# Block-local attention with global tokens: probabilities turned by SyncE's transposing DMAs, weighed two steps later, scores in two PSUM tiles, V in three pieces

## The reference

```python
# x: 4 x 1024 x 1024; 16 heads of 64; block 128; key window 256
h = layernorm(x)
q, k, v = h @ Wq + bq, h @ Wk + bk, h @ Wv + bv
# local: query block i sees keys 128*i - 64 .. 128*i + 192 (cut at the ends)
probs = softmax(q_block @ k_window.T / 8);  ctx = probs @ v_window
# global: row 0, row 1023 and the 62 rows of largest |q| of each head see all keys
g_ctx = softmax(q[idx] @ k.T / 8) @ v;      ctx[idx] = g_ctx
x = x + ctx
x = x + layernorm(x) @ (weight * scale_weight[:, None]).T + bias
```

## Time and profile before

| | us |
|---|---|
| median of 3 runs | 2138.94 (2134.4 to 2142.42) |
| profiled execution | 2139.94 |
| its span (first to last instruction) | 2138.4 |
| TensorE busy | 2105.3 (98%) |
| VectorE busy | 1347.3 (63%) |
| ScalarE busy | 750.6 (35%) |
| GpSimd busy | 502.7 (24%) |

### The profile page before, as it was taken

One profiled execution on the slowest core, in us unless ns is written; L12 is line 12 of the kernel. 1 busy time (PEld: TensorE's weight loads), 2 busy tenths in 40 slices (PEclk: granted clock), 3 DMA queues, 4 the chain that ended last, 5 costly groups with the idle time before them and its releaser, 6 DMA issues.

```text
span 2138.4 us, 36665 instructions
## 1 busy us (share of the span) xinstructions
PE 2105.3 (98%) x12576; PEld 1794.5 (84%) x12576; DVE 1347.3 (63%) x2615; ACT 750.6 (35%) x1915; POOL 502.7 (24%) x336
## 2 busy tenths in 40 slices
PE   6999999999999999999999999999999999999999
PEld 6878888888788888887888888888888888888887
DVE  5686666546966665459656655496555566666664
ACT  4334344442344344432444445224434451000000
POOL 2231121123411221243112311432123112212121
PEclk9999999999999999999999999999999999999999
DMA  4333232223332322233322221323223113333331
GB/s 161 104 95 92 75 104 67 61 69 99 107 90 75 106 60 65 69 95 93 98 85 77 84 70 42 103 65 86 65 68 123 51 58 134 140 131 134 137 128 69
DMA packets 192506, 194.29 MB, mean 91 GB/s; under 512 B 91984, under 2 KB 157590, under 8 KB 192400
## 3 DMA queue, kind: packets, MB, share of 16 engines
q1 hardware_dynamic: 184752, 175.19, 27.7%
q10 hardware_dynamic: 4320, 15.73, 1.8%
q0 software_dynamic: 3328, 2.17, 0.6%
HBM read 122.73 MB, written 51.44 MB: 81 GB/s over the span
## 4 chain that ended last, share of the span: by engine, by line
PE 85%; DVE 11%; issue 2%; DMA 1%; ACT 1%; DVEq 0%; SPq 0%; POOL 0%; ACTq 0%; POOLq 0%
PE proj L566 40%; PE proj L742 15%; PE pv L691 10%; PE score L664 5%; PE turn L679 5%; PE pv L722 3%; DVE top_idx L1307 2%; DVE x_norm L1309 2%; PE score L704 2%; DVE top_val L1305 2%; DVE q_sq L1272 2%; PE turn L714 1%; PE turn L731 1%; PE proj L831 1%; DVE norms L1274 1%
## 5 line engine op out<-in xcount | busy, mean ns | idle before, releaser
L566 PE MATMUL proj<-xT_hi,w_lo 128*128 128x512 f32 x1536 | 409.6, 398 | 0.0
L566 PE MATMUL proj<-xT_hi,w_hi 128*128 128x512 f32 x1536 | 402.7, 404 | 2.5 <-issue 1.5
L566 PE MATMUL proj<-xT_lo,w_hi 128*128 128x512 f32 x1536 | 381.5, 390 | 0.0
L434 POOL CAST w_hi<-w_raw 128x1024 fp32r<-128x1024 f32 x96 | 100.7, 1049 | 1178.4 <-PE proj L566 910.3
L566 PEld LDWEIGHTS proj<-xT_lo,w_hi 128*128 128x128 f32 x1536 | 288.6, 188 | 63.1
L566 PEld LDWEIGHTS proj<-xT_hi,w_lo 128*128 128x128 f32 x1536 | 281.1, 188 | 62.2 <-issue 0.2
L566 PEld LDWEIGHTS proj<-xT_hi,w_hi 128*128 128x128 f32 x1536 | 274.2, 188 | 63.4 <-DVE kT_lo L1290 2.7
L994 ACT ACTIVATE probs<-score,neg_max 128x256 f32<-128x256 f32 (+1 forms) x512 | 229.2, 460 | 183.4 <-DVE neg_max L1363 122.5
L691 PEld LDWEIGHTS pv<-v_nat,pT 128*128 128x128 f32 x2048 | 248.1, 191 | 10.4
L691 PE MATMUL pv<-v_nat,pT 128*128 128x64 f32 x2048 | 242.3, 271 | 0.0
L436 POOL TENSOR_TENSOR w_lo<-w_raw,w_hi 128x1024 fp32r<-128x1024 f32 x96 | 232.4, 2421 | 7.8
(11 more groups left out here) (165 smaller groups left out, 2975.0 us busy)
## 6 DMA issues: line engine op xcount, KB each, us to landing
w_raw<-in_wstream SPq DMA_DIRECT2D x96, 512.0 KB
x_buf<-in_rows SPq DMA_DIRECT2D x55, 512.0 KB, 4.1
q_rows<-q_nat SPq DMA_DIRECT2D x64, 256.0 KB
ctx_rows<-ctx_out SPq DMA_DIRECT2D x128, 128.0 KB, 1.8
q_store<-ctx_rows SPq DMA_DIRECT2D x30, 512.0 KB
out<-q_store ACTq DMA_DIRECT2D x30, 512.0 KB, 2.6
q_store<-in_cols SPq DMA_DIRECT2D x28, 512.0 KB
q_store<-in_rows SPq DMA_DIRECT2D x8, 512.0 KB, 5.3
```

What stands on the lines that cost most here:

```text
L434: pool.tensor_copy(w_hi[b][:, :], w_raw[b][:, :]).then_inc(w_hi_set, 1)
L566: mm = pe.matmul(proj[:, bank, :], w[b][:, k * P:k * P + P], x[:, k, half * HALF:half * HALF + HALF], start=(m == 0), stop=(m == 23), skip ...
```

## The change

**Turning.** TensorE's transposes of probabilities are gone, and with them ScalarE's copies out of `turn`. In their place, for each of the five events and each half (ten times a unit): VectorE splits the probabilities into 16-bit halves (`part_p`), SyncE issues a transposing DMA (`turn_p`, which is now SyncE's), and ScalarE joins the two halves into `pT` (`join_p`). `pT` becomes three tiles: two that alternate over the steps and `pT_g` for the global event. The buffers for it come from reuse: `v_parts` lies in `q_sq`, `q_nat` and `qT_cur` in the two `pT`.

**Order on TensorE.** A step is weighed about two steps after its scores. The weighings of step 3 and of the global event stand in the next unit. The scores of steps 1 and 3 go to the PSUM tile `turn`, which is free now; those of 0 and 2 to `score`.

**V and banks.** V goes in three equal pieces of 3 tiles each (`V_PIECES = 3`), all three joined within the second step. The parts of a unit come in the order V, V, K, K (V, K, V, K in unit 6), and each 512-token half has a seat (bank and count) given by `seat`: the first halves of V and K in bank 0, the second ones in bank 1, in most units.

**SyncE.** In `stores`, the loads of rows (units 0 and 1), of the last column (unit 2) and the linear layer's first loads (last batch, unit 7) stand between the transposes of step 1 and step 2; before, the row loads were the last of the unit. The store of step 3's context moves into the next unit, and the saving of the row statistics behind the last transposes of unit 3.

**VectorE.** The row moments stand in the middle of the unit instead of near its end; `SCALE_AT`, `LO_AT`, `HI_AT` and `AHEAD_AT` give other places.

The core of the diff:

```diff
+        v_parts = q_sq[:, 0:3 * P].bitcast(U16).rearrange("p (s x) -> p s x", s=2)
+        v_turned = sb("v_turned", [P, 3, 2, 3 * P], U16)
         v_nat = sb("v_nat", [P, TILES + 1, 2, HD])
-        probs = sb("probs", [P, SEQ])
-        pT = sb("pT", [P, SEQ + P])
+        probs = sb("probs", [P, SEQ + P])
+        p_parts, p_turned = (sb(name, [P, 2 * (SEQ + P)], U16) for name in ("p_parts", "p_turned"))
+        pT = [sb(f"pT{b}", [P, SEQ]) for b in range(2)]
+        pT_g = sb("pT_g", [P, SEQ + P])
+        q_nat, qT_cur = pT[0][:, :].rearrange("p (t d) -> p t d", d=P), pT[1]
...
+        score_of = [score, turn, score, turn]
...
+        V_PIECES = 3
+        V_NEEDS = (1, 2, 3, 3)
+
+
+        def half_words(s, h):
+
+            return slice(h * HALF, h * HALF + HALF + (P if s == STEPS and h == 1 else 0))
+
+
+        def pT_of(s):
+            return pT_g if s == STEPS else pT[s % 2]
+
+
+        BANK_USES = (SLICES + 1, SLICES - 1)
+
+
+        def seat_q(i, half):
+
+            return (1 - i, half) if i < 2 else (half, i)
+
+
+        def seat(what, j, half):
+
+            if isinstance(j, int) and j == 0:
+                return (0 if what == "v" else 1), PAIRS + half
+            if isinstance(j, int) and j == PAIRS - 1:
+                if what == "v":
+                    return 0, 3 * PAIRS - 2 + half
+                return ((1, 3 * PAIRS - 2), (0, 3 * PAIRS))[half]
+            return half, 2 * j + PAIRS + (0 if what == "v" else 1)
...
-        SCALE_AT = {(4, 1): (0,), (4, 2): (1,), (4, 3): (2,), (4, 6): (3,), (5, 1): (4,), (5, 2): (5,), (5, 3): (6,), (6, 1): (7,)}
+        SCALE_AT = {(4, 0): (0,), (4, 2): (1,), (4, 3): (2,), (5, 0): (3,), (5, 2): (4,), (5, 3): (5,), (6, 0): (6,), (6, 1): (7,)}
...
+            def turn_p(n, hp, s):
+
+                i = n * (PAIRS * EVENTS) + hp * EVENTS + s
+                for h in range(2):
+                    words = half_words(s, h)
+                    sp.wait_ge(p_parted, 2 * i + h + 3)
+                    apart(sp)
+                    sp.wait_ge(pT_set, 2 * i + h + 1)
+                    apart(sp)
+                    sp.dma_start_transpose(p_turned[:, 2 * words.start:2 * words.stop].rearrange("p (x r) -> p x r", r=P),
+                                           p_parts[:, 2 * words.start:2 * words.stop]).then_inc(p_moved[h], 16)
...
+                turn_p(n, hp, 0)
+                if hp > 0:
+                    store_ctx(n, hp - 1, STEPS - 1)
+                turn_p(n, hp, 1)
+                if hp == HALF_PAIRS + 1 and not following:
+                    load_ahead_next()
+                if hp < 2 and following:
+                    load_rows(n, hp + 2)
+                if hp == 2:
+                    load_last_column(n, following)
+                if last and not following:
+                    load_first()
+                turn_p(n, hp, 2)
                 store_ctx(n, hp, 0)
-                if hp < PAIRS - 1:
+                if not last:
                     turn_v(n, hp + 1, 0)
-                if hp == PAIRS - 1 and not following:
-                    load_first()
-                store_ctx(n, hp, 1)
                 if next_slices:
                     sp.wait_ge(w_split[1], n * BUFS + PAIRS // 2 + 3 + hp)
                     sp.dma_start(w_raw[1][:, :], next_slices[1]).then_inc(raw_in[1], 16)
+                turn_p(n, hp, 3)
+                store_ctx(n, hp, 1)
+                if not last:
+                    turn_v(n, hp + 1, 1)
+                turn_p(n, hp, STEPS)
                 store_ctx(n, hp, 2)
+                if not last:
+                    turn_v(n, hp + 1, 2)
                 if hp == HALF_PAIRS - 1 and following:
                     save_stats(n)
-                store_ctx(n, hp, 3)
-                if hp < PAIRS - 1:
-                    turn_v(n, hp + 1, 1)
+                if hp == HALF_PAIRS + 1 and not following:
+                    load_bias()
+                if last:
+                    store_ctx(n, hp, STEPS - 1)
...
-            def turn_p(u, s):
-                for h in range(2):
-                    pe.wait_ge(exp_set, 2 * (u * EVENTS + s) + h + 1)
-                    if s == 0:
-                        apart(pe)
...
-                            mm = pe.transpose(turn[0:rows, col:col + P], probs[:, src:src + rows], ident[:, :])
-                    mm.then_inc(p_turned, 1)
...
             def weigh(u, s):
                 pe.wait_ge(pv_free, u * EVENTS + s + 1)
-                if s < 2:
-                    pe.wait_ge(v_set, 2 * u + s + 1)
+                pe.wait_ge(v_set, u * V_PIECES + V_PIECES + V_NEEDS[s])
                 for h in range(2):
-                    pe.wait_ge(pT_set, 2 * (u * EVENTS + s) + h + 1)
+                    pe.wait_ge(pT_set, u * (2 * EVENTS) + 2 * s + h + 3)
...
+            def attend(n, hp):
                 u = n * PAIRS + hp
...
+                opens = isinstance(hp, int) and hp == 0
+                early = isinstance(hp, int) and hp == PAIRS - 2
+                scores(n, hp, 0)
+                part_of(n, hp, 0)
+                if not opens:
+                    weigh(u - 1, 3)
+                part_of(n, hp, 1)
+                scores(n, hp, 1)
+                if not opens:
+                    global_weigh(u - 1)
+                part_of(n, hp, 2)
+                scores(n, hp, 2)
+                part_of(n, hp, 3)
+                weigh(u, 0)
+                part_of(n, hp, 4)
+                scores(n, hp, 3)
+                turn_gq(u)
+                part_of(n, hp, 5)
+                weigh(u, 1)
+                if not early:
+                    part_of(n, hp, 6)
...
+                weigh(u, 2)
+                if early:
+                    part_of(n, hp, 6)
...
+            def join_p(n, hp, s, h):
+
+                i = n * (PAIRS * EVENTS) + hp * EVENTS + s
+                words = half_words(s, h)
+                act.wait_ge(p_moved[h], 16 * i + 32)
+                if s in (2, 3):
+                    act.wait_ge(pv_done, i - 1)
+                elif isinstance(hp, int) and hp == 0 and s == 0:
+                    act.wait_ge(q_stored[h], n * (16 * PAIRS) + 16 * PAIRS + 16)
+                    act.wait_ge(q_squared[h], n * PAIRS + PAIRS + 1)
+                apart(act)
+                act.copy(pT_of(s)[:, words].bitcast(U16).rearrange("p (x s) -> p s x", s=2),
+                         p_turned[:, 2 * words.start:2 * words.stop].rearrange("p (s x) -> p s x", s=2)).then_inc(pT_set, 1)
...
+                exps(u, 3, 0)
+                gq_hi_out(u)
+                before(3, 0)
+                exps(u, 3, 1)
+                before(3, 1)
+                if not last:
+                    out("v", 1, 2)
...
+            def part_p(n, hp, s, h):
+
+                i = n * (PAIRS * EVENTS) + hp * EVENTS + s
+                words = half_words(s, h)
+                dve.wait_ge(exp_set, 2 * i + h + 3)
+                dve.wait_ge(p_moved[h], 16 * i + 16)
                 apart(dve)
-                dve.tensor_copy(v_nat[:, V_TILES[h], :, :].rearrange("p t h d -> p (t h d)").bitcast(U16)
-                                .rearrange("p (t r s) -> p t s r", r=P, s=2), v_turned[:, V_TILES[h], :, :]).then_inc(v_set, 1)
+                dve.tensor_copy(p_parts[:, 2 * words.start:2 * words.stop].rearrange("p (s x) -> p s x", s=2),
+                                probs[:, words].bitcast(U16).rearrange("p (x s) -> p s x", s=2)).then_inc(p_parted, 1)
...
+                join_v(n, hp, 0)
+                top_norms(2)
+                part_p(n, hp, 1, 1)
+                inverses(u, 1)
+                for k in range(1, V_PIECES):
+                    join_v(n, hp, k)
...
+                part_p(n, hp, 2, 0)
+                top_norms(3)
+                pad_q(n, u, hp, half)
+                pv_out(u, 0)
+                part_p(n, hp, 2, 1)
+                inverses(u, 2)
+                if following and hp < HALF_PAIRS - 1:
+                    row_moments(n, hp + 1)
                 columns(2)
+                maxima(u, 3)
+                if not last:
+                    split_q(u + 1, hp + 1)
+                part_p(n, hp, 3, 0)
+                gq_lo_out(u)
+                if ahead:
+                    out_ahead(1, 0)
+                top_norms(4)
                 pv_out(u, 1)
-                if ahead:
-                    out_ahead(0, 0)
-                maxima(u, 3)
-                inverses(u, 2)
-                pad_q(n, u, hp, half)
-                top_norms(3)
+                part_p(n, hp, 3, 1)
+                inverses(u, 3)
+                if not last:
+                    part_v(n, hp + 1, 1)
```

677 lines of the change are left out of this document (357 added, 320 removed).

## The result

| | before | changed |
|---|---|---|
| median, us | 2138.0 (4 runs) | 2258.6 (2256.7 to 2263.5, 4 runs) |
| ratio, 95% interval | | 1.057 (1.054 to 1.059) |
| profiled execution, span | 2139.9, 2138.4 | 2260.1, 2258.4 |

What follows compares the result with a forecast made beforehand. TensorE's own work was taken to bound the kernel, end to end. From 2139.9 us, less 154.2 and 7.1, plus 24, 42, 9 and 11, came 2064.7, less 1 for the median: 2064 us, range 2035 to 2095.

Steps and rivals of the forecast that it cites:

- (a): TensorE's part after the second weighing waits for V's copy behind ScalarE's joins: 1.0 us in 24 units, 24 us.
- VectorE's term: VectorE gains ten splittings, loses 1 us in V's pieces: 32.4 us busy in a unit of 36.6, 88% full.
- (b): Units 0 to 2, first three batches: row loads ahead of third step's transposes in SyncE's queue; 42 us besides (a).
- What goes: TensorE's transposes of probabilities, 4.8 us a unit, 154.2 in all, and 7.1 us of waits at them.
- splittings at 0.69: VectorE's ten splittings of probabilities a unit, priced by its fast 1024-element row at 0.69 us each.
- joins at 1.0: ScalarE's ten joins a unit, priced between 0.6 and 1.12, taken as 1.0 us (0.95 back to back).
- The round trip: Splitting, DMA and join between scores and weighing: 8 us needed, about 17 available, so the weighing doesn't wait.
- (c): Unit 4, first three batches: late spreading of row statistics delays VectorE's scaling and maxima; 3 us more than (a), 9 us.
- The hand order: VectorE's operations in order with the forecast's prices; in unit 4 it waits until about 12 us in.
- VectorE sets the pace: Rival: VectorE, 88% full, has late maxima; each unit loses 1.5 us more, 48 us, time 2112; chance 0.15.
- transposes in series: Rival: transposing DMAs don't overlap, 3 us each, making a unit 44.5 us, time 2239; chance 0.08.

Runs made afterwards that it cites:

- e2: Changed kernel, ScalarE's copy of V's second half moved ahead of step 3's exponentials in units 0 to 6: 2193.8 us, ratio 1.027.
- e12: Changed kernel, GpSimd's subtraction for the weights' low parts in eight instructions of 128 columns instead of one of 1024: 2224.0 us, ratio 1.042.
- e9: Changed kernel, GpSimd's subtraction for V's and K's weight slices cut to 64 of 1024 columns, the rest left out: 2230.7 us, ratio 1.044.
- the better version: e8's kernel, roots and statistics store as in the changed kernel, unit 4's spreading load and first column scalings placed otherwise: 2182.4 us, ratio 1.021.
- e11: The better version, GpSimd's subtraction for V's and K's weight slices cut to 64 of 1024 columns: 2127.1 us, ratio 0.996.
- e8: Changed kernel, V's second copy earlier (not unit 6), statistics earlier, row loads apart, first query stores ahead of loads: 2165.0 us, ratio 1.013.
- e13: e8's kernel with GpSimd's subtractions in eight instructions of 128 columns, nothing left out: 2110.3 us, ratio 0.989.
- e1: Changed kernel, loads of rows (units 0, 1) and last column (unit 2) put back at the unit's end in SyncE's queue: 2252.1 us, ratio 1.055.
- e5: Changed kernel, row loads in units 0 and 1 cut from 1024 to 64 columns, their place in the queue kept: 2249.0 us, ratio 1.052.
- e15: Changed kernel, V's second copy ahead of step 3's exponentials (not unit 6) and GpSimd's subtractions in eight pieces: 2146.1 us, ratio 1.004.

## Why the prediction was wrong, step by step

The forecast was 195 us too low. The step that failed most is (a), the wait for V's copy behind the joins: the sum priced it at 1.0 us a unit, 24 in all; in units 3 and 5, where nothing else is in the way, it cost 4.1, and moving that copy alone gave back 65 us (e2), a part of it in units 0 to 2, where (b) waits for the same copy. The second is VectorE's term, which left out who shares with it: GpSimd's subtraction in pieces gave back 34 (e12). The third is (b), whose cause was right in one unit of three.

- *What goes, 154.2 + 7.1 us.* Right in kind, 7 us too large. The sum took 0.97 us for each of four turnings; the fourth occupies 0.79, from 642.61 to 643.40, so a unit loses 4.6 us and the kernel 147:

```profile
642.61 1.04 PE L679 MATMUL turn<-ident,probs 128*128 128x128 f32 x8
643.40 2.08 PE L566 MATMUL proj<-xT_hi,w_hi 128*128 128x512 f32 x8
```

That would leave 36.8 us a unit; unit 6 takes 37.1, against 36.6 forecast.
- *VectorE, splittings at 0.69.* Right where GpSimd is idle; it left out who shares with it. Splittings take 1.23 us beside GpSimd, and other operations of VectorE are held too; with the subtraction shortened 28 us came back in the changed kernel (e9) and 55 in the better version (e11).
- *ScalarE, joins at 1.0.* Mis-sized: 1.36. The row with the same count of elements moved four-byte ones; the bound of 1.12 was no bound for this copy, which writes every second 16-bit word (whether that is why wasn't tested). The Trainium skill ("ScalarE: Activation LUTs", section "What ACT_TABLE_LOAD costs") gives 186 ns and 0.833 per element for an ACTIVATE with immediate scale and bias, by which 1024 elements would be an estimated 1.04 us; this case's two sizes, 1.357 and 1.655 us for 1024 and 1280, rise by 1.16 ns per element, so the measurement decides.
- *The round trip, 8 us, weighings don't wait.* Right for this kernel: 8.3 us of waits for pT and 4.8 for pT_g. The other waits helped: where units come near 37 us, the wait for pT_g leads the list (49.5 us in e8, 33.1 in e13).
- *(a), 24 x 1.0 us.* The place was right to the line, the price four times too small: in units 3 and 5 it was 4.1 us (shown by e2, which gives it back). The wait was 2.24 instead of 0.95, from two joins (0.8) and maxima of VectorE that began late; most of the rest is the granted clock behind the wait. The sum priced waits as idle time alone; over the kernel the lower clock behind them is up to 79 us (estimated above).
- *(b), 42 us for row loads ahead of the third transposes.* Right for unit 0, which got 5 us shorter with the loads last (e1); wrong for units 1 and 2, which stayed about as long, and with short loads were 2 us shorter or less (e5). All told 6.5 us came back, not 42. With the loads last TensorE waits in these units for q_pad and v_nat, which VectorE writes, so VectorE's lateness stands behind the loads; that it makes up the rest is argued, not shown. V's copy in its right place and GpSimd in pieces bring units 0 to 2 to 38 to 45 us (e15), with the loads where they were, but that edit also takes V's copy off the path of (b).
- *(c), 9 us in unit 4.* Right chain, wrong size: 55.2 us a unit against some 40.5 forecast (36.6, 1 of (a) and 3). The hand order had VectorE wait until 12 us into the unit; it was 24, for the roots' second stage ended 5 us into unit 4, and both the store and the spreading load took longer than the one 6.5 us that was counted.
- *Nothing was priced at batch starts.* Unit 7 with the query phase takes 150.4 us, against 138.7 before and 134 by the sum. TensorE waits there 2.2 us for columns and 6.0 before the second turned queries, whose buffer now is one of the two pT; the copy ahead of it waits 8.8 us for the store of the first queries behind row loads. Storing first made TensorE's wait 2.4 us in place of 6.0 (e8); the rest of the 16 us wasn't taken apart.
- *Rivals.* "VectorE sets the pace" (0.15) had the mechanism that binds the better versions, though in the place of lateness at waits and not of a full engine: VectorE is at most 34.3 us busy in the units shown. The rival nearest in time, transposes in series (2239 us, 0.08), had the wrong mechanism: it made every unit 44.5 us, and unit 6 takes 37.1 with the same ten turnings; that its time is near is luck.

What stays open: how much of units 1 to 4 in e13 is the round trip of the global event (waits for pT_g) and how much VectorE's search; how units 1 and 2 of the changed kernel divide; and most of the 16 us at each batch's start.

## What to carry to other kernels

Price a wait of TensorE at more than its length: here 2.2 us cost 3.6, and some 80 of the lost us were matmuls at a lower clock. When a hop through three engines replaces work on the bottleneck, look at what each in-order queue holds behind the hop, not at the hop: moving one copy ahead of two joins that it didn't need gave back 65 us. And before giving VectorE more copies, see which GpSimd instruction runs beside them, and cut it into short ones; that paid even in the kernel before, by 0.4%.

## What the runs showed of the hardware

- A copy of VectorE in its fast form that begins behind a GpSimd subtraction stands still until that ends (2.60 us for 0.69); so do f32 operations with two inputs in SBUF (squares of 0.69 us: 1.12 on average, q's low part 3.30 for 1.22). Maxima don't. Eight GpSimd instructions of 128 columns took 4.3 us on average where one of 1024 took 2.5, and let VectorE in between.
- Splitting 1280 elements in 16-bit halves cost VectorE 1.49 us as 5 tiles before, and costs 0.82 as two equal halves where GpSimd is idle.
- ScalarE's interleaving copy of two-byte elements costs 1.357 us for 1024 and 1.655 for 1280, alone or beside GpSimd.
- Ten transposing DMAs of 256 KB a unit (one of them 320), next to 1.5 to 2.5 MB of loads, landed in 3.3 us (median); as plain copies they changed the time by 0.6%, within the noise of two runs.
- A store of 4 KB of statistics and the load that spreads them (512 KB) took 18 us in a row (811.3 to 829.7).
